# A four-layer graph network on one core: one written-out list for set-up and two groups, with new steady orders and banks

## The reference

```python
x = layernorm(x + attention(x, mask, adj))       # 8 heads of 64; softmax*0.33 + 0.33*adj + 0.33*exp(-adj)
x = layernorm(x + hypergraph(x, adj, W1, W2))    # conv, relu, layer norm, conv, + x; H = (adj != 0)
x = layernorm(x + relu(sum_k X_k @ Wk[k] + bk))  # X_{k+1} = T X_k, T = normalised adj * exp(leaky(s_j + s_i))
x = layernorm(x + relu([x, adj @ x / deg] @ W3.T))
```

## Time and profile before

| | us |
|---|---|
| median of 3 runs (1283.16 to 1285.7) | 1285.09 |
| profiled execution | 1283.25 |
| its span, first to last instruction | 1281.4 |
| PE, DVE, ACT, POOL busy in it | 1231.0, 1109.5, 959.2, 488.3 |

### The profile page before, as it was taken

One profiled execution on the slowest core, in us unless ns is written; L12 is line 12 of the kernel. 1 busy time (PEld: TensorE's weight loads), 2 busy tenths in 40 slices (PEclk: granted clock), 3 DMA queues, 4 the chain that ended last, 5 costly groups with the idle time before them and its releaser, 6 DMA issues.

```text
span 1281.4 us, 32306 instructions
## 1 busy us (share of the span) xinstructions
PE 1231.0 (96%) x9397; PEld 1092.4 (85%) x9397; DVE 1109.5 (87%) x3463; ACT 959.2 (75%) x2774; POOL 488.3 (38%) x1126
## 2 busy tenths in 40 slices
PE   4799999999999999999999999999999999999985
PEld 4588889888888888888988888898888898888874
DVE  3779889899889998988999998899898899999885
ACT  3567777778777777777777877778787777787773
POOL 2234333334343334433333444333443333344432
PEclk9889999999999999999999999999999999999998
DMA  8111101111110111111111111011111101111000
GB/s 227 30 23 40 39 21 26 30 38 38 38 28 25 28 32 38 38 38 21 25 30 38 38 38 29 25 28 32 38 38 38 23 23 30 38 38 30 16 10 9
DMA packets 146696, 45.14 MB, mean 35 GB/s; under 512 B 110577, under 2 KB 145521, under 8 KB 146673
## 3 DMA queue, kind: packets, MB, share of 16 engines
q1 hardware_dynamic: 142976, 43.81, 14.9%
q10 hardware_dynamic: 3520, 0.54, 0.3%
q0 software_dynamic: 176, 0.52, 0.2%
HBM read 36.45 MB, written 8.39 MB: 35 GB/s over the span
## 4 chain that ended last, share of the span: by engine, by line
PE 80%; DVE 6%; ACT 5%; issue 4%; POOL 3%; ACTq 2%; POOLq 0%; DVEq 0%
PE PS L434 13%; PE PS L435 13%; PE PS L438 13%; PE PS L563 5%; PE PS L553 5%; PE PS L509 4%; PE PS L543 4%; PE PS L510 4%; PE PS L513 4%; PE PS L598 3%; PE PS L612 2%; ACT mbc L864 2%; POOL rs L1720 1%; DVE ysb L1445 1%; ACT qk L875 1%
## 5 line engine op out<-in xcount | busy, mean ns | idle before, releaser
L1714 POOL TENSOR_TENSOR rs<-mv,eps_c 128x1 f32<-128x1 f32 x256 | 51.9, 203 | 640.3 <-DVE mv L1205 640.3
L1720 POOL TENSOR_TENSOR rs<-rs,mhalf 128x1 f32<-128x1 f32 x320 | 175.9, 550 | 25.4
L892 ACT ACTIVATE prob<-PS,neg_max 128x128 f32<-128x128 f32 x512 | 179.7, 383 | 2.0 <-DVE neg_max L1277 2.0
L509 PE MATMUL PS<-xT_hi,wqk_hi 128*128 128x256 f32 x512 | 144.5, 304 | 4.6 <-ACT wv_hi L837 4.6
L1290 DVE SCALAR_TENSOR_TENSOR prob<-prob,rl,gate 128x128 f32<-128x128 f32 x512 | 143.7, 342 | 0.1
L510 PE MATMUL PS<-xT_hi,wqk_lo 128*128 128x256 f32 x512 | 135.6, 286 | 0.0
L892 ACT ACTIVATION_READ_ACCUMULATOR prob<-PS,neg_max 128x1 f32 x512 | 114.3, 223 | 0.0
L509 PEld LDWEIGHTS PS<-xT_hi,wqk_hi 128*128 128x128 f32 x512 | 98.7, 193 | 9.9 <-issue 5.1
L1727 POOL TENSOR_SCALAR rs<-mv,rs 128x1 f32<-128x1 f32 x256 | 84.1, 329 | 53.1 <-POOL rs L1720 53.1
L513 PE MATMUL PS<-xT_lo,wqk_hi 128*128 128x256 f32 x512 | 103.9, 285 | 0.0
L510 PEld LDWEIGHTS PS<-xT_hi,wqk_lo 128*128 128x128 f32 x512 | 99.4, 194 | 0.0
(11 more groups left out here) (223 smaller groups left out, 4194.9 us busy)
## 6 DMA issues: line engine op xcount, KB each, us to landing
xin<-in_x_dram SPq DMA_DIRECT2D x32, 256.0 KB, 2.7
out_dram<-xout SPq DMA_DIRECT2D x32, 256.0 KB, 2.2
xblk<-in_x_dram SPq DMA_DIRECT2D x124, 64.0 KB, 2.4
ablk<-in_adj_dram SPq DMA_DIRECT2D x128, 32.0 KB, 1.9
adj_in<-in_adj_dram SPq DMA_DIRECT2D x32, 128.0 KB, 2.1
wrow<-in_adj_dram SPq DMA_DIRECT2D x32, 128.0 KB, 4.5
wqkv_raw<-in_L_gnn_W_qkv_dram SPq DMA_DIRECT2D x1, 1536.0 KB, 7.7
w_raw<-in_L_gnn_W_dram SPq DMA_DIRECT2D x3, 512.0 KB, 10.6
```

Of the source, the lines that this page charges most:

```text
L509: pe.matmul(dst, w[0], xT0[0][:, c], start=(c == 0), stop=False)
L892: last = act.activation(prob[:, t, h, :], PS[:, bank, k * P:(k + 1) * P], ACT.Exp, bias=neg_max[:, t, h:h + 1], accum_out=row_sum[:, t, h: ...
L1720: return pool.tensor_tensor(rs[:, n, g, 1:2], rs[:, n, g, 0:1], mhalf[:], ALU.pow)
```

## The change

**One list.** `first`, `group(0)`, `set_up_done` and `group(1)` give way to one function `head()` on each engine. It holds the set-up and groups 0 and 1 in a new order, with the waits it needs. The loop starts at group 2 as before, and a last call `group(ITERS + 1)` is added, since the outputs of group s - 2 now come in `group(s)`.

**Set-up work moved.** GpSimd takes the spreading of gamma and beta, the centring of W3, the small gate vectors and the sum of the three biases. ACT forms W3's row sums by copies with an accumulated sum and clears `gate_c` with a copy of zero scale, now its first operation. The low part of W_out comes before those of W1. TensorE's two row products become two steps.

**Requests.** gamma and beta go from ACT's queue to GpSimd's, Wv from ACT's to SP's; on ACT's queue nodemask goes behind the x blocks; SP's order is new.

**Steady order.** All four `group` lists are reordered, and `bank_...` is new almost throughout. `norm_` signals each head, and `PT_` waits for each head. `mcol_` is separated from `incidence`.

```diff
+        bank_qk = (1, 6, 4, 5)
+        bank_v = (0, 5)
+        bank_PT = (2, 0)
+        bank_y0 = (4, 7)
+        bank_y1 = (5, 3)
+        bank_Z2 = (6, 2)
+        bank_T3 = (7, 6)
...
         def _(sp):
             (W_qkv)
+            (adj_in, mask_bc8, W1, W2, xin, W_out, W3, wrow)
-            (W2, W1)
             (ablk, four requests)
-            (adj_in, mask_bc8, wrow, xin)
             (Wk, three requests)
-            (W3, W_out)
+            (Wv)
             (aw, bv, ab, bk)
...
         def _(act):
-            act.dma_start(mask8[:], nodemask).then_inc(ld_mask, 16)
             for k in range(QB):
                 act.dma_start(xblk[k * Q:(k + 1) * Q], x_block(0, k)).then_inc(xb_in, 16)
-            (beta_c, gamma_c, wv2_raw)
+            act.dma_start(mask8[:], nodemask).then_inc(ld_mask, 16)
...
             def PT_(i, t):
-                    if h % (HEADS // 2) == 0:
-                        pe.wait_ge(dve_attn, 2 * (i * G + t) + 1 + h // (HEADS // 2))
+                    pe.wait_ge(dve_attn, HEADS * (i * G + t) + h + 1)
...
+            def w3_mean(o, t):
+                act.wait_ge(ld_w3, 16)
+                half = w3_raw[:, o, t * D:(t + 1) * D]
+                act.activation(half, half, copy, accum_out=w3m[:, o, t:t + 1]).then_inc(set_w3m, 1)
...
+            def centre_w3(o, t):
+                pool.wait_ge(set_small, 1)
+                settle(pool)
+                half = w3_raw[:, o, t * D:(t + 1) * D]
+                pool.tensor_scalar(half, half, w3m[:, o, t:t + 1], None, ALU.add).then_inc(set_w3c, 1)
```

More of the change, by code:

```diff
@@ L805, in first @@
-                pe.wait_ge(set_lo, W3_DONE - len(POOL_SPLITS))
+                pe.wait_ge(set_lo, 12)
+                qk_(1, 3)
                 ax_(0, 1)
[L808 to L811, removed]
+                h_(0, 0)
+                h_(0, 1)
+                S_(1, 0)
+                hT_(0, 0)
+                hT_(0, 1)
+                S_(1, 1)
+                hw_(0, 0)
+                hw_(0, 1)
+                y1_(0, 0)
+                v_(1, 0)
@@ new lines, in head @@
+                PV_(1, 1)
+                W_(1, 0)
+                pe.wait_ge(act_qk, 10)
+                T2_(0, 1)
+                xT3_(0, 0)
+                W_(1, 1)
+                xT3_(0, 1)
+                Z3_(0, 0)
+                AT_(1)
+                Z3_(0, 1)
+                T3_(0, 0)
+                qk_(2, 2)
+                T3_(0, 1)
+                ax_(1, 0)
+                ax_(1, 1)
+            pe.wait_ge(ident_ok, 2)
+            pe.wait_ge(pool_const, 9)
+            head()
@@ new lines, in bw_copy, with high @@
+            def bw_copy():
+                act.wait_ge(set_pe, SET_BW)
+                act.activation(bw_bc[:], PS[:, bank_bw, 0:D], copy).then_inc(set_copy, 1)
+            def high(n):
+                src, hi, lo, factor, (ready, value) = splits[n]
+                act.wait_ge(ready, value)
+                if factor is None:
+                    act.activation(hi, src, copy).then_inc(set_hi, 1)
+                else:
+                    act.activation(hi, src, copy, scale=factor).then_inc(set_hi, 1)
@@ new lines, in head @@
+                gate_(2)
+                OT_(1, 0)
+                Y_(0, 0)
+                PT_(1, 1)
+                Y_(0, 1)
+                OT_(1, 1)
+                qk_(2, 1)
+                x2_(0, 1)
+                BHT_(1)
+                carry(1)
+                xT3_(0, 0)
+                xT3_(0, 1)
+                Z3_(0, 0)
+                x3_(0, 0)
+                AT_(1)
+                Z3_(0, 1)
+                x1_(1, 0)
+                x1_(1, 1)
+                x3_(0, 1)
@@ L1112, in _ @@
+                ax_(1, 0)
+            zero_gate()
+            act.wait_ge(pool_const, 9)
+            head()
             with act.Fori(2, ITERS - 1) as s:
@@ L1115, in _ @@
             group(ITERS)
+            group(ITERS + 1)
         @block.vector
@@ L1650, in first @@
+                low(15)
+                deg_(1)
+                incidence(1)
                 Dn_(0)
+                cnt_(1)
                 ax_(0, 0)
                 ax_(0, 1)
-            first()
-            group(0)
-            set_up_done(dve)
-            group(1)
+                dve.wait_ge(ld_vec, 48)
+                hb_(0, 0)
+                dve.wait_ge(set_pool_lo, 2)
+                hb_(0, 1)
+                max_(1, 0)
+                bnh_(0, 0)
+                hT_(0, 0)
@@ new lines, in head @@
+                mvh_(0, 0)
+                bnh_(0, 1)
+                mvh_(0, 1)
+                rl_(1, 0, 0)
+                dve.wait_ge(set_small, 4)
+                hT_(0, 1)
+                hw_(0, 0)
+                max_(1, 1)
+                y1_(0, 0)
+                hw_(0, 1)
+                norm_(1, 0, 0)
+                low(16)
+                rl_(1, 0, 1)
+                low(17)
+                y1_(0, 1)
+                bn1_(0, 0)
+                norm_(1, 0, 1)
+                rl_(1, 1, 0)
```

780 lines of the change are left out of this document (458 added, 322 removed).

## The result

The changed kernel takes 1255.7 us (median of 4 runs, 1253.9 to 1256.34); the kernel before took 1284.12 beside it. The ratio is **0.9776, 95% interval 0.9759 to 0.9793**: 28.4 us less. The forecast was 1268.7, 16.4 us less, with a range down to 1259: the sign was right, the gain is 1.7 times the forecast and lies outside the range. The profiled execution took 1253.9, 29.35 less than that of before (1283.25).

The account below looks back on a forecast made before the run. TensorE was taken to bound the steady group, with gains before 73 us and in its remaining loop wait. Head -9.2 (2.0 - 12.7 + 1.5) and loop -7.2 gave -16.4: 1266.85, or 1268.7 us on the median's level, range 1259 to 1282.

Parts of the forecast that it names:

- The start, +2.0: Before the first qk product: 0.7 MB more passes ahead of x, so qk starts 2.0 us later, at 20.8.
- qk to h, -12.7: First qk product to h of group 0, 54.4 us before: shorter waits and fewer slow-clock stretches, 12.7 us less in sum.
- The waits: Qk to h: DVE relief -4.1, oT_hi hole -4.6, end-of-group gaps -3.2, later exp(0,0) +1.6, column_sums +1.0 us.
- The clock, -3.4: Qk to h: with fewer TensorE gaps, one of three half-clock stretches stays; full clock elsewhere gives back 3.4 us.
- W3's part: Qk to h, within the -4.1: W3's sum (1.2 us) and centring (1.1) leave a DVE that ran without a break.
- Group 1, +1.5: Group 1, 32.4 us, TensorE full: extra DVE and GpSimd work delays hw(0,1) and v(1,1), 1.5 us more, bounds 0 and 3.
- The loop, -0.25 a group: Steady groups: copying qk(s,3) before the mask ends the wait in S, at most -0.4; -0.25 taken, -7.2 us over 29 groups.
- the moved outputs: Loop: outputs and their scale go one group on, onto a GpSimd busy 15.03 of 37.8 us; priced at 0.
- PT by single heads: Loop: listed among the new waits of the walk, PT waiting head by head, with no price.
- the loop gains nothing: Rival, chance 0.20: S's wait goes but ax or T1 takes it up; only the head gains, 1275.9 us.
- The margin of 0.05 us at x1t: Loop: x1t of graph 1 comes 0.05 us before ax wants it, so -0.25 was taken instead of -0.4.
- The tail, 0: After the loop: the same chain with some ACT work added under h, no change, within 1 us.

Follow-up runs that it names:

- after_again: The changed kernel measured once more, unedited, as the control of the start experiments: 1255.52 us, ratio 0.9779 to the kernel before.
- before_warm: Kernel before plus 74 transposes of the identity, results unread, in four TensorE gaps: 1280.76 us, ratio 0.9981.
- after_w3_dve: Changed kernel with W3's sums, scale and centring given back to DVE: 1257.84 us, ratio 0.9804 to the kernel before.
- before_qk3_early: Kernel before with ACT's copy of qk(s,3) moved ahead of the second half of the mask: 1284.08 us, ratio 1.0002.
- before_act_half: Kernel before with only ACT's order changed: gate_ and the qk(s,3) copy ahead of the masks, second output behind them: 1270.03 us, ratio 0.9897.
- after_qk_first: Changed kernel with nodemask requested first, SP holding until W_qkv landed, first three qk ahead of W1's transposes: 1247.96 us, ratio 0.9723 to kernel before.
- after_hold: Changed kernel with nodemask requested first and SP holding all requests after W_qkv until x landed: 1252.71 us, ratio 0.976 to kernel before.
- after_mask_first: Changed kernel with nodemask requested ahead of x on ACT's queue: 1256.6 us, ratio 0.979 to the kernel before.
- after_qk3_late: Changed kernel with ACT's copy of qk(s,3) put back behind mask and second output: 1255.79 us, ratio 0.9777 to kernel before.
- after_pt_half: Changed kernel with PT waiting for four heads at a time again: 1263.27 us, ratio 0.9836 to the kernel before.

## Why the prediction was right in sign and wrong in size

- **The start, +2.0**: +3.6 (18.77 to 22.35; +4.6 in after_again). The mechanism held in the main: nearly equal turns (q1 2632 packets beside q10's 2192; 2695 beside 2720 before), x late, DVE behind mask8. The term that was mis-sized is the bytes that pass ahead of x: I had put 0.7 MB more, 2.0 us. By the rows above it was 1.03 MB more (4.31 less 3.28), all of it SP's, and x landed 3.2 us later; the other 0.4 us are mask8, 0.3 behind x, and its conversion.
- **qk to h, -12.7**: -17.9. The waits were near: -9.3 in the working (-4.1, -4.6, -3.2, +1.6, +1.0), -11.1 measured. column_sums waits 1.35 us (+1.0 was taken); gate vector, W3's transposes and oT_hi are in time. **The clock, -3.4, is the step that failed**: TensorE's own work fell by 6.8, close to the whole 6.2 of the three stretches. I had let one of them stay by judgement, without asking the walk where a gap ahead of it would be left; it left none but column_sums, and no fall of the clock follows that one. The inverse holds in part: in before_warm the clock alone gave 3.0 in the stretch, as long as the waits stood. W3's part was priced at DVE's time, 2.3; in after_w3_dve the stretch is 3.5 longer, with the clock behind the wait. The working also took the 0.87 of the earlier trace rows for the whole stretch; that no clock record covers its first 3.0 us, and that their products are slow, it did not see.
- GpSimd's pass was taken at 0.73 us, by the sum of two tiles; the centring took 1.10 each. It was hidden.
- **Group 1, +1.5**: +1.2 (33.63 less 32.41), but this was luck: the late hw and v of the working would show as idle time, and there is 0.16. 0.36 us of it are the four products of AT of group 1, which `head()` has ahead of the first T3 and the kernel before behind it; the first distance of the loop gives them back. The rest are small holds spread over the group, not taken apart.
- **The loop, -0.25 a group**: -0.51 (37.80 to 37.29), and 16.2 us over the loop where 7.2 stood. **This is the largest miss, and the second step that failed.** "TensorE's only wait there is in S ... at most -0.4 a group" counted one wait as the stall and the copy's place as its cause. The size of that stall was about right (0.3 and 0.1 taken, 0.43 measured from S to `hT_`); its cause was not. The wait that shows is the first consumer of a late row of ACT work; behind it `hid` was just as late. The edit that I named as the cause is worth nothing by itself (before_qk3_early, distance 37.81), and ACT's order as a whole is worth 0.45 (before_act_half). The working did not price what ACT's 0.77 us for the scale, before the masks, cost the row, and it called the moved outputs 0; by ACT's rows that move carries the gain, though no run isolates it.
- "PT by single heads" was listed as a new wait only, with no price. It is worth 0.22 a group in the new lists and nothing beside the better ACT order in the old ones.
- The rival *the loop gains nothing* (S's wait goes, another takes it up) is what one of the edits does alone, with `hid` in place of ax or T1. The margin of 0.05 us at x1t, for which I cut the term, did not bind: ACT reaches both x1t without a gap in its new list.
- **The tail, 0**: 0.0.

## What to carry to other kernels

A wait on the critical engine can name just the first consumer of a late row, and not the instruction that made the row late: before pricing it, look back along the releasing engine for its last idle time, and at the next consumer behind. A wait and a half clock behind it can come as a pair: price a gap with the clock it may bring (2.1 us brought 1.5 more in after_w3_dve, the 1.35 us at column_sums brought none), and count the clock back only where no other wait takes it up. Where the bound engine is full from its first product on, most of a microsecond saved at the start arrives at the end, so hold back the transfers that nobody needs yet and let the first products go ahead of work for later stages.

## What the runs showed of the hardware that was not expected

- beta and gamma, element by element, took ACT 5.85 and 2.37 us to issue; the same two requests took GpSimd 0.77 and 0.99.
- ACT's fourth request for x took 3.93 us to issue (3.9 to 4.6 in five executions with nodemask last) and nodemask behind it 3.19; with nodemask first, the fourth took 0.69 to 0.76 in the three variants of the changed kernel that have it so. The requests are the same five; why their order matters was not tried.
- The first qk products take 0.41 us each for a form that takes 0.28 later, and the change comes where the trace's clock record begins: at 18.59 us in after_qk_first, 21.73 in the kernel before, 23.93 in after_hold, 25.86 in the changed kernel. From the first qk product to that point it is 4.1, 3.0, 1.45 and 3.5 us, and 5.55 in before_warm and 5.8 in after_mask_first. In after_qk_first the first 36 products took 6.37 us, in after_hold, right behind the W1 transposes, 5.20. So a difference of one or two microseconds at the start can be the clock's and not the edit's.
- In after_again, after_mask_first, after_qk3_late and after_pt_half the last of the loop's distances is 38.1 to 38.2 us instead of 36.7. In each of the four the granted clock falls there (0.72 in 1200 to 1206 us in after_again and after_qk3_late, 0.74 in after_mask_first, 0.86 in 1206 to 1218 us in after_pt_half); in the first profile of the changed kernel it does not (1.00). One and the same kernel ran with the fall and without it.
